# Two stages of a mixture-of-experts kernel made one: results gathered while padding tiles still run

## The reference

```python
aff = softmax(an @ router_w + router_b)            # an: (tokens, 256), 31 experts
topv, topi = top_k(aff, 3)
gates = sum(one_hot(topi) * topv)                  # (tokens, 31)
h = gelu(einsum('bsd,edh->besh', an, re_w1) + re_b1)
routed = einsum('bse,besh,ehd->bsd', gates, h, re_w2) + einsum('bse,ed->bsd', gates, re_b2)
out = shared + routed + an + attn_out
```

## Time and profile before

| | us |
|---|---|
| median of three runs | 1179.06 |
| the profiled execution | 1180.83 |
| its span (first to last instruction) | 1179.1 |
| PE busy / DVE busy / POOL busy | 957.7 / 709.0 / 499.6 |

### The profile page before, as it was taken

One profiled execution on the slowest core, in us unless ns is written; L12 is line 12 of the kernel. 1 busy time (PEld: TensorE's weight loads), 2 busy tenths in 40 slices (PEclk: granted clock), 3 DMA queues, 4 the chain that ended last, 5 costly groups with the idle time before them and its releaser, 6 DMA issues. The chain is left out here.

```text
span 1179.1 us, 21213 instructions
## 1 busy us (share of the span) xinstructions
PE 957.7 (81%) x5518; PEld 704.7 (60%) x5519; DVE 709.0 (60%) x2039; ACT 547.6 (46%) x1383; POOL 499.6 (42%) x673
## 2 busy tenths in 40 slices
PE   4785899995398998948999999979983599999631
PEld 2444555563275666737767667657862489998510
DVE  7754566666676778657777677722455834443344
ACT  1225688885234334327777777722330045554300
POOL 5001333335387686841123333422001466666375
PEclk9797999998598988979999999989997589999855
DMA  5675844434356675869777777737437144448444
GB/s 174 221 265 162 228 126 127 122 111 138 107 190 236 251 253 193 315 232 233 214 195 198 206 201 201 198 108 202 141 118 240 42 115 131 131 133 126 92 131 118
DMA packets 162731, 204.15 MB, mean 173 GB/s; under 512 B 23842, under 2 KB 104513, under 8 KB 162658
## 3 DMA queue, kind: packets, MB, share of 16 engines
q1 hardware_dynamic: 150898, 179.64, 49.4%
q0 software_dynamic: 6048, 16.52, 6.9%
q10 hardware_dynamic: 5712, 7.13, 2.1%
HBM read 121.34 MB, written 81.76 MB: 172 GB/s over the span
## 5 line engine op out<-in xcount | busy, mean ns | idle before, releaser
L816 DVE CUSTOM_DVE_ANT_0 a_sm<-a_sc,keep_mask_qk 128x512 f32<-128x512 f32 (+3 forms) x256 | 118.3, 482 | 64.6 <-PE a_sc L732 57.5
L599 DVE CUSTOM_DVE_ANT_0 a_junk<-a_sc,keep_mask_qk 128x512 bf16<-128x512 f32 (+3 forms) x256 | 110.9, 487 | 68.4 <-PE a_sc L501 67.8
L481 POOL TENSOR_SCALAR_AFFINE_SELECT a_probs<-a_probs 128x128 f32<-128x128 f32 (+1 forms) x192 | 63.4, 331 | 193.8 <-ACT a_probs L569 193.7
L804 ACT ACTIVATE a_probs<-a_sm,a_neg 128x512 f32<-128x512 f32 (+3 forms) x256 | 140.1, 551 | 8.7 <-DVE a_neg L816 8.6
L731 PE MATMUL a_sc<-a_ka,a_qa 128*128 128x512 f32 (+3 forms) x256 | 96.3, 377 | 26.9 <-POOL a_ka L713 18.0
L1146 POOL TENSOR_TENSOR rope_rot<-rope_wqkv 128x512 f32<-128x512 f32 x64 | 93.2, 1471 | 56.4 <-DVE rope_wqkv L1221 56.3
L713 POOL CAST a_ka<-a_ka 64x512 fp32r<-64x512 f32 x64 | 38.9, 607 | 178.0 <-DMA a_qa<-qs 172.4
L737 PE MATMUL a_tp<-keep_ident,a_probs 128*128 128x128 f32 x640 | 104.5, 280 | 0.0
L1737 POOL DMA_INDIRECT ex_xg<-an,ex_idc x78 | 79.3, 1016 | 58.7 <-POOL ex_idc L1734 56.5
L569 ACT ACTIVATE a_probs<-a_st 128x512 f32<-128x512 f32 (+1 forms) x192 | 95.2, 525 | 17.2 <-PE a_st L505 15.7
L1809 DVE COPY ex_w<-keep_w 128x514 f32 x78 | 36.6, 469 | 93.0 <-ACT ex_hid L1793 90.6
(11 more groups left out here) (252 smaller groups left out, 2148.5 us busy)
## 6 DMA issues: line engine op xcount, KB each, us to landing
a_qa<-qs SPq DMA_DIRECT2D x128, 128.0 KB, 3.3
ks<-rope_rot SPq DMA_DIRECT2D x56, 256.0 KB, 2.6
qs<-rope_rot SPq DMA_DIRECT2D x56, 256.0 KB, 2.4
ye<-ex_y SPq DMA_DIRECT2D x78, 128.0 KB, 2.3
qs<-rope_roth SPq DMA_DIRECT2D x32, 256.0 KB, 2.5
vs<-rope_vout SPq DMA_DIRECT2D x16, 512.0 KB, 3.3
ks<-rope_roth SPq DMA_DIRECT2D x32, 256.0 KB, 3.6
a_ka<-ks SPq DMA_DIRECT2D x64, 128.0 KB, 3.4
```

The lines of the kernel that those rows point to most:

```text
L599: return dve.tensor_tensor_reduce(out=junk[:, JUNK[qb]:JUNK[qb] + n], in0=src, in1=c.mask_qk[:, S - n:S], scale=1.0, scalar=-3e38, op0=ALU ...
L804: act.activation(probs[:, h % PR, rows(qb)], sm[:, h % SM, rows(qb)], ACT.Exp, bias=neg[:, h % 2, qb:qb + 1], scale=-1.0, accum_out=sums[: ...
L816: return dve.tensor_tensor_reduce(out=sm[:, h % SM, rows(qb)], in0=src[:, 0:n], in1=c.mask_qk[:, S - n:S], scale=-1.0, scalar=3e38, op0=AL ...
```

## The change

The stages `experts` and `combine` become one.

* The three loops of four steps are written out as 78 steps on every engine.
* POOL no longer copies row numbers; it gathers by `c.ids` directly, into a ring `xg` of 12 tiles instead of 4. It may run 12 tiles ahead of the transposes.
* After its 78 gathers POOL reads the number of real tiles from `c.experts` (`route` writes it to the last column) and waits until so many tiles are stored (`ye_done`). Then it issues the 48 gathers of `ye`.
* These go to a ring of ten output tiles, `y`. Its last four places are the memory of `xg`: before output tile 6 (`FREE`) POOL waits for all 78 transposes.
* SP counts stored tiles: in step n it stores tile n, waits for the store of tile n - 2 and raises `ye_done`.
* DVE makes the gates in steps 8 to 12 of the tile loop. The gate transposes and bias products stand behind PE's last tile. In the sum for an output tile the bias is now added last.
* `attention1` gets a new transfer on SP, between `inputs_stored(B)` and the loop: it fills the rows of tiles 48 to 77 of `ye` with zeros, 128 x 30 pieces of 1 KB. The new stage waits for it before its first store.

```diff
             inputs_stored(B)
+            least = TOK * TOPK // P
+            rest = t["ye"].rearrange("(p n) d -> p n d", n=NT)[:, least:NT, :]
+            sp.dma_start(rest, c.mask_qk[:, 0:D].rearrange("p (o d) -> p o d", o=1).to_broadcast([P, NT - least, D])).then_inc(c.ye_set, 16)
             with sp.Fori(PEELED, PASSES) as it:
...
-            dve.tensor_copy(c.experts[:, :], row_b[0:1, 0:P]).then_inc(slots_known, 1)
+            dve.tensor_copy(c.experts[:, 0:NT], row_b[0:1, 0:NT]).then_inc(slots_known, 1)
+            dve.tensor_copy(c.experts[:, P - 1:P], ct[0:1, E - 1:E]).then_inc(slots_known, 1)
...
+        XR, YR, RING = 12, 4, 10
+        FREE = RING - XR // TOPK
+        ADDS = TOPK + 1
+        y = a.sb("y", [P, RING, TOPK, D])
+        xg = y[:, FREE:RING, :, :].rearrange("p i k d -> p (i k) d")
...
         def _(pool):
-            def step(it, r):
-                sl = r % 4
-                ge(pool, turned, it, 4, r - 3)
-                pool.tensor_copy(idc[:, sl:sl + 1], c.ids[:, bass.ds(4 * it + r, 1)]).then_inc(id_set, 1)
-                ge(pool, id_set, it, 4, r + 1)
-                pool.nop(nofuse=True)
-                pool.indirect_dma_start(out=xg[:, sl, :], out_offset=None, in_=t["an"],
-                                        in_offset=bass.IndirectOffsetOnAxis(ap=idc[:, sl:sl + 1], axis=0)).then_inc(gathered[sl], 16)
-
-            steps(pool, step, NT - 1)
+            for n in range(NT):
+                ge(pool, turned, n - XR + 1)
+                pool.indirect_dma_start(out=xg[:, n % XR, :], out_offset=None, in_=t["an"],
+                                        in_offset=bass.IndirectOffsetOnAxis(ap=c.ids[:, n:n + 1], axis=0)).then_inc(gathered[n % XR], 16)
+
+            tiles = pool.value_load(c.experts[0:1, P - 1:P], min_val=TOK * TOPK // P, max_val=NT)
+            pool.wait_ge(ye_done, tiles)
+            pool.wait_ge(gate_ready, 1)
+            pool.nop(nofuse=True)
+            for i in range(TILES):
+                if i == FREE:
+                    pool.wait_ge(turned, NT)
+                ge(pool, summed, ADDS * (i - RING + 1))
+                for k in range(TOPK):
+                    pool.indirect_dma_start(out=y[:, i % RING, k, :], out_offset=None, in_=t["ye"],
+                                            in_offset=bass.IndirectOffsetOnAxis(ap=c.slots[:, k, i:i + 1], axis=0))\
+                        .then_inc(fetched[i % RING], 16)
 
         @block.sync
         def _(sp):
...
+            sp.dma_start(b2[:, :], t["L0_ffn_re_b2"]).then_inc(b2_in, 16)
+            sp.wait_ge(c.ye_set, 16)
+            for n in range(NT + 2):
+                if tile(n):
+                    sp.wait_ge(y_copied, n + 1)
+                    sp.dma_start(ye[n], ysb[:, n % YR, :]).then_inc(stored[n % YR], 16)
+                if n >= 2:
+                    sp.wait_ge(stored[(n - 2) % YR], 16 * ((n - 2) // YR + 1))
+                    sp.nop(nofuse=True).then_inc(ye_done, 1)
...
+            pe.wait_ge(gate_ready, 1)
+            pe.wait_ge(x_copied, NT)
+            for b in range(B):
+                ge(pe, g_copied, b - 1)
+                for i in range(SB):
+                    mm = pe.transpose(tb[b % 2][0:E, P * i:P * i + P], gate[:, SB * b + i, :], c.ident[:, :])
+                mm.then_inc(g_turned, 1)
+            pe.wait_ge(b2_in, 16)
+            for i in range(TILES):
+                pe.wait_ge(g_copied, i // SB + 1)
+                ge(pe, summed, ADDS * (i - 1))
+                pe.matmul(bb[i % 2][:, 0:D], gateT[:, P * i:P * i + P], b2[:, :], start=True, stop=True).then_inc(b_mul, 1)
...
+                if r >= 8:
+                    gate_part(r - 8)
             for i in range(TILES):
+                dve.wait_ge(fetched[i % RING], 16 * TOPK * (i // RING + 1))
                 for k in range(TOPK):
+                    ge(dve, summed, ADDS * i + k)
                     dve.scalar_tensor_tensor(out=c.base[:, i, :], in0=y[:, i % RING, k, :], scalar=c.gates[:, i, k:k + 1],
                                              in1=c.base[:, i, :], op0=ALU.mult, op1=ALU.add).then_inc(summed, 1)
+                dve.wait_ge(b_mul, i + 1)
+                dve.wait_ge(summed, ADDS * i + TOPK)
+                dve.tensor_add(c.base[:, i, :], c.base[:, i, :], bb[i % 2][:, 0:D]).then_inc(summed, 1)
```

More of the change, by code:

```diff
@@ L1696, in experts @@
         xT, hid = a.sb("xT", [P, 2, DC, P]), a.sb("hid", [P, 2, MC, P])
[L1697 to L1702, removed]
@@ L1703, in experts @@
-        block = a.stack.enter_context(nc.Block())
[L1705 to L1721, removed]
@@ L1723, in there @@
-        def there(it, r):
-            return not isinstance(it, int) or 0 <= 4 * it + r < NT
-        ye = t["ye"].rearrange("(p n) d -> n p d", n=NT)
+        ysb = a.sb("ysb", [P, YR, D])
+        gate, gateT = a.sb("gate", [P, TILES, E]), c.ow[0:E, :, :].rearrange("p k n -> p (k n)")
+        b2 = a.sb("b2", [E, D])
+        tb, hb, yb, bb = ([a.ps(f"{n}{i}") for i in range(2)] for n in ("tb", "hb", "yb", "bb"))
+        gathered = [a.sem(f"gathered{i}") for i in range(XR)]
+        stored = [a.sem(f"stored{i}") for i in range(YR)]
@@ new lines, in experts @@
+        fetched = [a.sem(f"fetched{i}") for i in range(RING)]
+        turned, x_copied, w_copied, h_mul, h_done, y_mul, y_copied, ye_done = (a.sem(n) for n in (
+            "turned", "x_copied", "w_copied", "h_mul", "h_done", "y_mul", "y_copied", "ye_done"))
+        summed, out_s, b2_in, picked_k, gate_ready, g_turned, g_copied, b_mul = (a.sem(n) for n in (
+            "summed", "out", "b2_in", "picked", "gate_ready", "g_turned", "g_copied", "b_mul"))
+        block = a.stack.enter_context(nc.Block())
@@ L1752, in _ @@
+            for i in range(TILES):
+                sp.wait_ge(summed, ADDS * (i + 1))
+                sp.dma_start(out[i // SB, P * (i % SB):P * (i % SB) + P, :], c.base[:, i, :]).then_inc(out_s, 16)
+            sp.wait_ge(out_s, 16 * TILES)
         @block.tensor
         def _(pe):
-            def step(it, r):
-                if there(it, r):
-                    sl = r % 4
-                    ge(pe, gathered[sl], it, 16, 16)
-                    ge(pe, x_copied, it, 4, r - 1)
+            for r in range(NT + 2):
+                if tile(r):
+                    pe.wait_ge(gathered[r % XR], 16 * (r // XR + 1))
+                    ge(pe, x_copied, r - 1)
@@ L1795, in step @@
                     mm.then_inc(h_done, 1)
[L1796 to L1802 removed]
+                n = r - 2
+                if tile(n):
+                    act.wait_ge(y_mul, n + 1)
+                    ge(act, stored[n % YR], 16 * (n // YR))
+                    act.activation(ysb[:, n % YR, :], yb[n % 2][:, 0:D], ACT.Copy).then_inc(y_copied, 1)
@@ L1814, in _ @@
-            steps(dve, step, NT - 1)
-def combine(nc, c, t, out):
-    a = Alloc(nc, "cb")
-    with a.stack:
-        RING = 4
-        y = a.sb("y", [P, RING, TOPK, D])
-        picked, gate = a.sb("picked", [P, TOPK, TILES, E]), a.sb("gate", [P, TILES, E])
-        gateT = a.sb("gateT", [E, TOK])
-        b2 = a.sb("b2", [E, D])
-        gt_b, bb = ([a.ps(f"{n}{i}") for i in range(2)] for n in ("gt", "bb"))
-        gathered = [a.sem(f"gathered{i}") for i in range(RING)]
-        summed, out_s, b2_in, tick_s, gate_ready, g_turned, g_copied, b_mul = (a.sem(n) for n in (
-            "summed", "out", "b2_in", "tick", "gate_ready", "g_turned", "g_copied", "b_mul"))
-        block = a.stack.enter_context(nc.Block())
-        ADDS = TOPK + 1
-        @block.gpsimd
-        def _(pool):
+                if r >= 8:
+                    gate_part(r - 8)
@@ L1965, in program @@
         route(nc, c, t)
-        experts(nc, c, t)
-        combine(nc, c, t, out)
+        experts(nc, c, t, out)
 def kernel(**inputs):
```

134 lines of the change are left out of this document (46 added, 88 removed).

## The result

| | us |
|---|---|
| before, median of five runs | 1179.06 (1178.14 to 1180.85) |
| after, median of five runs | 1189.68 (1186.16 to 1192.07) |
| after / before | 1.0084, 95% interval 1.0061 to 1.0106 |
| forecast | 1157.5, range 1148 to 1167 |
| the profiled execution after, and its span | 1190.7 and 1189.0 |

A forecast was written before the change was run, and what follows sets the result against it. PE was taken to bound the experts and POOL `combine`, one after the other. First result gather at 1075.3, last gather starting at 1139.7 and the tail gave 1148.0; plus 9.5 for the fill, 1157.5 us, range 1148 to 1167.

The forecast's parts named there:

- The step that failed: Tile loop: with 12 ring places the padding tiles' stalls go, and transpose 77 comes at 1095.5 instead of 1098.78.
- Rival D: First attention: the fill, reading the same bytes 30 times, takes 51 us; PE stalls 48, end 1196; chance 5%.
- Rival E: Result gathers do not start early, as `ye_done` comes only with the last tiles: first about 1104, end 1184; chance 2%.
- The start of the stage: First tile gather, without the row-number copy, at 939.8 instead of 940.38; steps 1.7 us earlier together (1.9 earlier to 0.6 later).
- The 1.1 us of the second transpose: Start of the tiles: the second transpose, which waited for its gather until 946.08, gains 1.1 us from denser gathers.
- The fill: First attention: zero fill ahead of head 16's loads takes 11.7 us of all engines and costs 9.5, stall clock's +1 included.
- Rival B: First attention: the fill is hidden, its writes interleaving with the loads within PE's 4.3 us slack; 1148 to 1150; chance 15%.
- The first result gather: Merged stage: POOL starts gathering results at 1075.3 (1074.8 to 1077), before the fill's cost, against 1109.84.
- Rival C: Result gathers: DVE's weight copies hold POOL their whole 0.47 us and later gathers lie in adds; 1165; chance 14%.
- What was called hidden: End of the stage: DVE needs 32 us from 1104.6, done at 1137, eight before POOL lets it.
- the 3 us for gathers inside adds: Result gathers: one inside DVE's adds takes 1.16 us, not 0.95; +3 allowed, between today's +1.8 and +6 for all.
- the 1.25 for a pause for code: POOL's result gathers: one pause for code, +1.25 us, as in the kernel before.

The follow-up runs named there:

- ahead4: Changed kernel, but POOL waits for transpose n - 4 before gathering tile n, so 4 tiles ahead and not 12: 1176.69 us.
- pace_ye: Changed kernel with a small POOL copy, a wait for it and a nop before each of the first 18 result gathers: 1174.47 us.
- static_pe: Changed kernel, but PE takes expert 0's second weight for every tile and reads no expert number; on chip 1: 1155.79 us.
- all_three: Changed kernel with the fill moved to `route`, POOL 4 tiles ahead, and full pauses before the first 18 result gathers: 1171.36 us.
- ramp_again: Changed kernel with fill in `route`, lead growing from 4 to 12 tiles, full pause before 14 result gathers; repeat run on chip 7: 1155.99 us.
- busy1: Changed kernel with one POOL memset before each of the first 18 result gathers, its waits long over; on chip 12: 1179.40 us.
- static_again: The kernel of `static_pe` run again unaltered, on chip 7: 1195.94 us.
- run 765: Not a run number: 765 counts the gather signal records, of 2016, in the first run of the unaltered changed kernel, 1189.68 us.

## Why the prediction was wrong, point by point

In the profiled execution transpose 77 came at 1135.13; the forecast's was 1095.5 + 9.5 = 1105.0, the last transpose plus the fill. The 30.1 us between are 2.5 less for the fill, 1.5 more since the steps began hardly earlier, 11.8 for the first stall and 19.3 for the second: 1105.0 - 2.5 + 1.5 + 11.8 + 19.3 = 1135.1. From there to the end it took 53.9 instead of 52.5.

* **The step that failed** is "with 12 places a gather of 5 us is never late. Transpose 77 comes at 1095.5", with "Gathers then follow every 1.25 to 1.3 us" before it. The distances were right. What the prediction took for granted is that a gather costs nothing to the engines that it doesn't feed. In every execution of the changed kernel that was profiled, PE's signals come late beside the dense gathers: 31 us, shown by ahead4 and pace_ye, each of which removes the stall beside its own gathers and leaves the other. The cost to PE's signals was put at nothing without a reason.
* **That the trace of before could have shown it** I don't think: in the experts a gather went out every 1.98 us, above the turn, and the dense ones of `combine` run beside a PE that gives one signal per output tile; all 16 of those signals are recorded within 0.02 us of the product's end. A rival "an engine's signals get late" was missing; of the slower cases, D and E held 7%, and neither is what happened.
* **The start of the stage** was to gain 1.7 us. POOL's first gather started 2.01 us behind the row-number cast, against 2.33 before, and the first transpose 5.20 us behind it against 5.41: 0.2 gained. The 1.1 us of the second transpose didn't come either: without a stall transposes 0 to 6 took 13.21 us (`static_pe`) against 13.39 before.
* **The fill** was mis-sized only: 7.0 us in this pair of traces, about 6 in the mean of all, against 9.5, inside the bounds of 0 and 11.6. One term of it was misread: a mean clock of 0.91 over 20 us means 3.6 us at the lower level (1.2 GHz), which cost 1.8; the text calls the 1.8 the time at that level. The sum had +1 for it. It landed in 19.7 us, the DMA share beside it was 1.05, and PE waited on the rows of zeros, as said. Rival B, the hidden fill, is out.
* **The first result gather**, the most important time of the forecast, was right given the two delays ahead of it (1094.3 against 1095.85). Rival E is out.
* **Rival C**, POOL held by DVE's copies, is out. In `static_pe` on chip 1, where nothing stalls, ten result gathers overlap a weight copy of 0.43 us for 0.3 us or more; they took 1.03 us in the mean and 1.13 at most, against 0.95 alone, and the first 18 starts were 1.32 us apart, as forecast (1.33). A gather that waited out the copy would have taken 0.95 + 0.43 = 1.38. The Trainium skill (SBUF — State Buffer, SBUF: two separate sides) says that such a fp32 copy keeps GpSimd from writing descriptors for the whole instruction; the durations of these gathers don't bear it out.
* **Rival D**, a fill at the price of the padding gathers, is out: 3840 pieces landed in 19.7 us with the loads beside them, and the cost was 7 us.
* **What was called hidden** wasn't: "DVE would be done at 1137, eight before POOL lets it". The bias product's signal came at 1152.83, after 15.33 us of waiting, and from there DVE with 2.15 us per output tile (2.0 in the forecast) sets the end. The note that DVE "is the next bound if POOL were faster" named the right engine for another reason.
* **The rest of the sum holds where the signals aren't late.** On chip 1 three kernels with all parts of the change, fill included, took 1153.5 to 1155.8, each with an edit that touches PE, the bytes or 0.1 us per gather. The forecast was 1157.5. In `static_pe` the first result gather came at 1085.08, where the forecast with its fill has 1084.8, and from there to the last gather it took 60.8 us instead of 64.4: most of the 3 us for gathers inside adds and the 1.25 for a pause for code weren't needed. The unaltered kernel never came to that chip, so what it takes there is argued and not shown.

What stays open is why the chips differ, and what in a dense row of gathers holds PE's signals. It isn't a fixed delay per gather. In `all_three` on chip 0 and `ramp_again` on chip 7 the dense row begins only when PE's tiles are done (1122.00 and 1104.45), and the bias products' signals that are recorded inside it come 0.02 us behind their product. In `busy1` on chip 12 and `static_again` on chip 7 the dense row begins beside tiles and runs on, and they come up to 3.9 us late. So density alone isn't enough; that PE must be giving several signals per step when the row begins fits these four, but wasn't tested. Nor was it tried with another engine in PE's place; ACT's signals to PE were prompt.

The traces differ in one more way, stall or no stall. A gather raises its semaphore 16 times, so the 126 gathers of the stage should leave 2016 records of it. The four traces of chip 1 hold 1996 to 2011 of them and the trace of the kernel before all 2016; the 14 of chips 0, 7 and 12 hold 708 to 974, and the changed kernel's first run 765. In those 15 they are missing from the first 10 us of the gathers on (53 to 63 records where chip 1 has 96) and none before the stage; in the stage, records of PE's, ACT's and DVE's signals are missing too. The profile's answers show it by a landing time that is there or not (`static_pe`'s tile gathers, then the changed kernel's first 18 result gathers):

```profile
DMA to landing us min/median/max: 2.7/3.1/5.1
...
ex_y<-ye,keep_slots POOLq DMA_INDIRECT x18
```

So `ramp_again` and `all_three`, which have no stall, still show that they ran on a chip of the stalled kind. The gap in the records also leaves a rival open. Every timed execution has a span and a granted clock on record, so none is known to have run without being recorded, and it may be the recording, on these chips, that holds the signals up. No run tells. A gap called "issue" in the rows above can be a signal whose record is missing: PE's 5.26 us before 1112.28 were a wait for the gelu. Last, chip 1 was used in one session only, so a cause that belongs to the session and not to the chip isn't excluded.

## What to carry to other kernels

Before an engine that issues gathers is let run ahead, ask at what rate it will then issue: a lead that grows slowly (here 4 tiles to 12) and a small pause where other engines trade signals took away the 31 us of stalls, and the time is 2% below the kernel before. A wait that ends on no instruction of the engine it waits for ("remote", "another core or an unknown queue") on a kernel with one core was a late signal here; look at what another engine is doing at that time. And when unlike edits remove the same stall in a place that they don't touch, suspect the machine and run the unaltered kernel again before believing any of them.

## What the runs showed of the hardware

* With gathers of 128 pieces issued by POOL 1.25 to 1.34 us apart beside the tiles, signals of PE began to reach ACT and DVE late (by 0.8 us and more) 8 to 12 us into the row at the start of the tiles and 1.3 to 3.5 us into the row at their end. They were late by up to 17.6 us in the changed kernel, and all came within 4 us of the row's end. At 1.52 us apart it took 11 us until one was more than 1.1 us late; at 1.77, 1.94 and 1.96 it didn't occur in 18 gathers. A quarter of the bytes changed nothing.
* It occurred on chips 0, 7 and 12 in all twelve traces whose gathers were dense beside the tiles, and on chip 1 in none of the three. The kernel before takes the same on both kinds (medians of 1176.7 to 1180.8 us), so its time doesn't tell them apart; the share of missing signal records in the merged stage does.
* Signals from ACT to PE in the same stalls took 0.14 us (gelu's end 1112.14, product 1112.28).
